# The first batch's layer norm in two halves, with new orders for the engines' instruction lists

## The reference, cut to what matters

```python
q, k, v = xn @ Wq.T, xn @ Wk.T, xn @ Wv.T
attn = softmax((q @ k.T) * tril / sqrt(512))     # masked scores are 0, not -inf: they count in the sum
gates = softmax(xn @ Wg); the 2 largest of 8, renormalized
out = x + attn @ v + sum over e of gate[e] * (xn @ We[e] + be[e])
```

## Time and profile before

| what | value |
|---|---|
| median of 3 runs | 120.28 us |
| profiled execution | 120.22 us |
| its span | 118.5 us |
| granted TensorE clock | 1.00 of full speed, throughout |
| busy TensorE matmul / weight load | 112.7 / 103.5 us |
| busy VectorE / ScalarE / GpSimd | 106.4 / 99.0 / 91.3 us |

### The profile page before, as it was taken

One profiled execution on the slowest core, in us unless ns is written; L12 is line 12 of the kernel. 1 busy time (PEld: TensorE's weight loads), 2 busy tenths in 40 slices (PEclk: granted clock), 3 DMA queues, 4 the chain that ended last, 5 costly groups with the idle time before them and its releaser, 6 DMA issues.

```text
span 118.5 us, 2933 instructions
## 1 busy us (share of the span) xinstructions
PE 112.7 (95%) x733; PEld 103.5 (87%) x733; DVE 106.4 (90%) x532; ACT 99.0 (84%) x338; POOL 91.3 (77%) x183
## 2 busy tenths in 40 slices
PE   4986999999999999999999999999999999999990
PEld 4965879998999989998899989999899989899990
DVE  0689999989999899999999899999999898998892
ACT  2456899899897999899997989899997989978930
POOL 7349569899768996699768995799868995896970
PEclk9999999999999999999999999999999999999999
DMA  3759500000300011000300020000300030000033
GB/s 95 255 165 304 157 3 6 0 3 3 89 0 3 0 55 39 0 0 3 94 3 0 0 68 20 6 0 3 94 0 0 0 90 4 0 3 0 6 91 89
DMA packets 9233, 5.18 MB, mean 44 GB/s; under 512 B 384, under 2 KB 9088, under 8 KB 9216
## 3 DMA queue, kind: packets, MB, share of 16 engines
q1 hardware_dynamic: 8656, 4.66, 13.6%
q10 hardware_dynamic: 560, 0.33, 1.0%
HBM read 2.89 MB, written 2.10 MB: 42 GB/s over the span
## 4 chain that ended last, share of the span: by engine, by line
PE 87%; DMA 4%; ACT 3%; DVE 2%; SPq 1%; issue 1%; DVEq 0%
PE ring L248 15%; PE ring L252 14%; PE ring L249 14%; PE attb L306 13%; PE score L293 8%; PE score L252 4%; PE score L249 4%; PE score L248 4%; DMA w_f<-in_w_stacked_dram 4%; PE ring L324 3%; PE ring L345 2%; PE attb L358 1%; PE ring L335 1%; PE ring L337 1%; PE ring L334 1%; ACT c_s L906 1%
## 5 line engine op out<-in xcount | busy, mean ns | idle before, releaser
L922 ACT ACTIVATE ysc<-ring,gate 128x128 f32<-128x128 f32 x124 | 35.6, 388 | 0.8 <-PE ring L252 0.6
L248 PE MATMUL ring<-w_hi,xT_hi 128*128 128x512 f32 (+2 forms) x96 | 35.5, 370 | 0.4 <-ACT xT_hi L1001 0.4
L249 PE MATMUL ring<-w_lo,xT_hi 128*128 128x512 f32 (+2 forms) x96 | 32.5, 339 | 0.0
L252 PE MATMUL ring<-w_hi,xT_lo 128*128 128x512 f32 (+2 forms) x96 | 32.5, 338 | 0.0
L1130 POOL TENSOR_TENSOR ysc<-ysc,mix 128x256 f32<-128x256 f32 x31 | 22.9, 738 | 6.2 <-DVE mix L576 3.6
L1127 POOL TENSOR_TENSOR ysc<-ysc 128x256 f32<-128x256 f32 x31 | 22.8, 736 | 6.0 <-ACT ysc L922 6.0
L576 DVE SCALAR_TENSOR_TENSOR mix<-ring,gate,mix 128x128 f32<-128x128 f32 x65 | 22.4, 347 | 0.9 <-PE ring L252 0.3
L306 PE MATMUL attb<-c_s,probT 128*128 128x128 f32 x152 | 21.8, 274 | 0.0
L306 PEld LDWEIGHTS attb<-c_s,probT 128*128 128x128 f32 x152 | 20.1, 191 | 0.2
L248 PEld LDWEIGHTS ring<-w_hi,xT_hi 128*128 128x128 f32 x96 | 18.1, 189 | 2.1 <-ACT xT_hi L1001 0.6
L252 PEld LDWEIGHTS ring<-w_hi,xT_lo 128*128 128x128 f32 x96 | 18.1, 188 | 1.5 <-DVE xT_lo L509 0.2
(11 more groups left out here) (115 smaller groups left out, 237.8 us busy)
## 6 DMA issues: line engine op xcount, KB each, us to landing
x_all<-in_x_dram SPq DMA_DIRECT2D x7, 256.0 KB, 3.9
out_dram<-o_s SPq DMA_DIRECT2D x7, 256.0 KB, 2.3
w_f<-in_w_stacked_dram SPq DMA_DIRECT2D x1, 256.0 KB, 4.5
w_f<-in_w_stacked_dram SPq DMA_DIRECT2D x1, 192.0 KB, 4.4
w_f<-in_w_stacked_dram SPq DMA_DIRECT2D x1, 132.0 KB, 3.7
x_all<-in_x_dram ACTq DMA_DIRECT2D x1, 128.0 KB, 2.7
x_all<-in_x_dram SPq DMA_DIRECT2D x1, 128.0 KB, 2.5
wqk_s<-in_w_attention_dram ACTq DMA_DIRECT2D x1, 128.0 KB, 3.9
```

The source lines that it names most:

```text
L248: nc.tensor.matmul(dst, hi, w_h, start=True, stop=False)
L249: nc.tensor.matmul(dst, hi, w_l, start=False, stop=False)
L252: return nc.tensor.matmul(dst, lo, w_h, start=False, stop=True)
L922: last = nc.scalar.mul(ysc[:, t, e, :], bank(f"A{t}", b)[:, e * P:(e + 1) * P], gate[:, b % 2, t, e:e + 1])
```

## The change

First batch: `normal_finish(0)` becomes `first_finish(0)` after tiles 0 and 1 and `first_finish(1)` after tiles 2 and 3. Each aggregates two tiles and adds EPS to two columns. GpSimd's power becomes two powers of two columns each (`first_rstd`). VectorE normalizes tile 0 before it makes the low part of the C weights and tiles 1 to 3 behind it; tiles 0 and 1 need only the first power. The negated mean of batch 0, which nothing read, is no longer made. The same diff gives new orders to all four lists and to the ring's groups; in the first part that moves, among others, `wb_high` to the front of ScalarE's list, two of batch 1's statistics ahead of `x_lo_half(0, 1)`, `u_hi(0)` ahead of `c_copy(0, 1)`, and `bias_rhs_split` ahead of `wa_low` on GpSimd. The instructions are otherwise the same. The diff, without the last parts of VectorE's and ScalarE's lists:

```diff
--- before.py
+++ after.py
@@ -53,8 +53,8 @@
 
 
 FIRST_GROUPS = """C0@0 C1@0 U@0 C2@0 C3@0 SV@0 B0@0 A0@0 X@1 A1@0 B1@0 U@1 C0@1 A2@0 C1@1 C2@1""".split()
-GROUPS = "B2- C3 A3- B3- SV DT- B0 A0 X+ A1 B1 U+ C0+ C1+ A2 C2+".split()
-LAST_GROUPS = """B2@-2 C3@-1 A3@-2 B3@-2 A0@-1 B0@-1 DT@-2 B1@-1 B2@-1 A1@-1 A2@-1 B3@-1 SV@-1 DT@-1 A3@-1""".split()
+GROUPS = "B2- C3 A3- B3- SV DT- A0 B0 X+ A1 B1 U+ C0+ C1+ A2 C2+".split()
+LAST_GROUPS = """B2@-2 C3@-1 A3@-2 B3@-2 A0@-1 DT@-2 B0@-1 B1@-1 A1@-1 B2@-1 B3@-1 A2@-1 SV@-1 A3@-1 DT@-1""".split()
@@ -398,14 +398,13 @@
             wide(0, "C", 3)
             value_sums(0)
             scores(0, 0)
+            wide(0, "B", 0)
             scores(0, 1)
-            wide(0, "B", 0)
             scores(0, 2)
             wide(0, "A", 0)
             transpose_x(1)
             transpose_probs(0, 0)
             wide(0, "A", 1)
-            transpose_probs(0, 1)
             scores(0, 3)
             wide(0, "B", 1)
             project_u(1)
@@ -413,25 +412,26 @@
             wide(0, "A", 2)
             attend(0, 0)
             wide(1, "C", 1)
+            transpose_probs(0, 1)
             wide(1, "C", 2)
 
             for n in range(1, B - 1):
                 wide(n - 1, "B", 2)
                 wide(n, "C", 3)
+                scores(n, 0)
                 attend(n - 1, 1)
-                scores(n, 0)
                 transpose_probs(n - 1, 2)
                 wide(n - 1, "A", 3)
+                wide(n - 1, "B", 3)
                 transpose_probs(n - 1, 3)
-                wide(n - 1, "B", 3)
+                scores(n, 1)
                 attend(n - 1, 2)
                 value_sums(n)
-                scores(n, 1)
                 transpose_rows(n - 1)
                 attend(n - 1, 3)
                 bias(n - 1)
+                wide(n, "A", 0)
                 wide(n, "B", 0)
-                wide(n, "A", 0)
                 scores(n, 2)
                 transpose_probs(n, 0)
                 transpose_x(n + 1)
@@ -439,43 +439,43 @@
                 wide(n, "B", 1)
                 scores(n, 3)
                 project_u(n + 1)
+                transpose_probs(n, 1)
                 wide(n + 1, "C", 0)
+                wide(n + 1, "C", 1)
                 attend(n, 0)
-                transpose_probs(n, 1)
-                wide(n + 1, "C", 1)
                 wide(n, "A", 2)
                 wide(n + 1, "C", 2)
 
             wide(B - 2, "B", 2)
+            transpose_probs(B - 2, 2)
             wide(B - 1, "C", 3)
+            attend(B - 2, 1)
             scores(B - 1, 0)
-            transpose_probs(B - 2, 2)
             wide(B - 2, "A", 3)
             wide(B - 2, "B", 3)
             transpose_probs(B - 2, 3)
             wide(B - 1, "A", 0)
             scores(B - 1, 1)
+            attend(B - 2, 2)
+            scores(B - 1, 2)
             transpose_probs(B - 1, 0)
+            transpose_rows(B - 2)
             wide(B - 1, "B", 0)
-            attend(B - 2, 1)
-            scores(B - 1, 2)
-            transpose_rows(B - 2)
+            wide(B - 1, "B", 1)
             scores(B - 1, 3)
-            wide(B - 1, "B", 1)
-            attend(B - 2, 2)
+            wide(B - 1, "A", 1)
             wide(B - 1, "B", 2)
             attend(B - 2, 3)
-            wide(B - 1, "A", 1)
+            wide(B - 1, "B", 3)
             bias(B - 2)
+            transpose_probs(B - 1, 1)
+            transpose_probs(B - 1, 2)
             wide(B - 1, "A", 2)
-            wide(B - 1, "B", 3)
-            transpose_probs(B - 1, 1)
             value_sums(B - 1)
-            transpose_probs(B - 1, 2)
+            wide(B - 1, "A", 3)
+            attend(B - 1, 0)
             transpose_probs(B - 1, 3)
-            attend(B - 1, 0)
             transpose_rows(B - 1)
-            wide(B - 1, "A", 3)
             attend(B - 1, 1)
             attend(B - 1, 2)
             bias_early(B - 1)
@@ -499,10 +499,18 @@
                     last = nc.vector.bn_aggr(mv[:, t, :], stats[:, t, :])
                 chain.step(last)
 
-                if b > 0:
-                    dve.wait_ge(S["rstd_ready"], b)
+                dve.wait_ge(S["rstd_ready"], b)
                 nc.vector.tensor_scalar_add(veps[:], mv[:, :, 1], EPS).then_inc(S["veps_ready"], 1)
                 nc.vector.tensor_scalar(nmean[:], mv[:, :, 0], -1.0, None, ALU.mult).then_inc(S["nmean_ready"], 1)
+
+            def first_finish(h):
+
+                dve.wait_ge(S["stats_ready"], 2 * h + 2)
+                for t in (2 * h, 2 * h + 1):
+                    last = nc.vector.bn_aggr(mv[:, t, :], stats[:, t, :])
+                chain.step(last)
+                two = slice(2 * h, 2 * h + 2)
+                nc.vector.tensor_scalar_add(veps[:, two], mv[:, two, 1], EPS).then_inc(S["veps0_ready"], 1)
 
             def split_lo(dst, src, hi, done):
 
@@ -703,6 +711,18 @@
 
             early, late = slice(0, 2 * P), slice(2 * P, NT * P)
 
+            def c_low(b):
+
+                dve.wait_ge(S["wc_ready"], 1)
+                split_lo(w_lo[:, c_cols], w_f[:, c_cols], w_hi[:, c_cols], S["wcl_ready"])
+
+            def xn_first(b, t):
+
+                if t % 2 == 0:
+                    dve.wait_ge(S["rstd_ready" if t else "rstd_early"], 1)
+                nc.vector.tensor_scalar(xn[:, t, :], tile_ap(0, t), mv[:, t, 0:1], rstd[:, t:t + 1], ALU.subtract,
+                                        ALU.mult).then_inc(S["xn0_ready"], 1)
+
             def a_low(b):
 
                 dve.wait_ge(S["ah_ready"], 1)
@@ -729,38 +749,37 @@
                 if t % 2 == 0:
                     dve.wait_ge(S["x0_late" if t else "x0_early"], 16)
                 normal_stats(0, t)
-            normal_finish(0)
-            dve.wait_ge(S["wc_ready"], 1)
-            split_lo(w_lo[:, c_cols], w_f[:, c_cols], w_hi[:, c_cols], S["wcl_ready"])
-            dve.wait_ge(S["rstd_ready"], 1)
-            for t in range(NT):
-                nc.vector.tensor_scalar(xn[:, t, :], tile_ap(0, t), mv[:, t, 0:1], rstd[:, t:t + 1], ALU.subtract,
-                                        ALU.mult).then_inc(S["xn0_ready"], 1)
-
+                if t % 2:
+                    first_finish(t // 2)
+            xn_first(0, 0)
+            c_low(0)
+            xn_first(0, 1)
+            xn_first(0, 2)
+            xn_first(0, 3)
             a_low(0)
             x_lo_half(0, 0)
             first_sums(0)
+            normal_stats(1, 0)
+            normal_stats(1, 1)
             x_lo_half(0, 1)
-            normal_stats(1, 0)
-            token_sums_pairs(0)
-            normal_stats(1, 1)
             normal_stats(1, 2)
             normal_stats(1, 3)
+            token_sums_pairs(0)
+            token_sums_later(0)
             normal_finish(1)
-            token_sums_later(0)
             u_lo(0)
             gate_max(0)
+            mask_scores(0, 0)
             gate_drop(0)
-            mask_scores(0, 0)
+            negate_max(0, 0)
             mask_scores(0, 1)
             gate_below(0)
-            negate_max(0, 0)
+            sv_rows(0, 0)
             negate_max(0, 1)
-            sv_rows(0, 0)
+            gate_sum(0)
             sv_rows(0, 1)
-            gate_sum(0)
+            gate_rec(0)
             sv_rows(0, 2)
-            gate_rec(0)
             gate_out(0)
             mix_b(0, 0, 0)
             mix_b(0, 0, 1)
@@ -775,108 +794,108 @@
                 negate_max(n - 1, 2)
                 mix_b(n - 1, 1, 2)
                 u_lo(n)
+                mask_scores(n - 1, 3)
                 normal_stats(n + 1, 0)
                 normal_stats(n + 1, 1)
                 normal_stats(n + 1, 2)
-                mask_scores(n - 1, 3)
+                negate_max(n - 1, 3)
                 mix_b(n - 1, 2, 0)
                 mix_b(n - 1, 2, 1)
-                negate_max(n - 1, 3)
+                mask_scores(n, 0)
                 mix_b(n - 1, 2, 2)
                 gate_max(n)
-                normal_stats(n + 1, 3)
                 gate_drop(n)
                 softmax_sum(n - 1)
+                normal_stats(n + 1, 3)
+                softmax_tot(n - 1)
                 token_sums_pairs(n)
-                softmax_tot(n - 1)
-                token_sums_later(n)
                 gate_below(n)
                 normal_finish(n + 1)
+                token_sums_later(n)
+                softmax_rec(n - 1)
+                negate_max(n, 0)
                 mix_b(n - 1, 3, 0)
-                mask_scores(n, 0)
+                gate_sum(n)
                 mix_b(n - 1, 3, 1)
-                gate_sum(n)
-                negate_max(n, 0)
+                gate_rec(n)
                 mix_b(n - 1, 3, 2)
-                gate_rec(n)
-                softmax_rec(n - 1)
                 gate_out(n)
                 mask_scores(n, 1)
                 sv_rows(n, 0)
                 sv_rows(n, 1)
+                finish_tile(n - 1, 0)
+                sv_rows(n, 2)
                 mix_b(n, 0, 0)
-                sv_rows(n, 2)
```

(38 more changed lines are left out.)

65 lines of the change are left out of this document (33 added, 32 removed).

## The result

The changed kernel takes 120.82 us (median of 5 runs, 120.65 to 121.02), the kernel before 120.28 in the same five rounds. The ratio is 1.0048 with a 95% interval of 1.0033 to 1.0063: slower by 0.4 to 0.76 us, outside the range given and on the other side.

What follows compares the result with a forecast made beforehand. TensorE was taken to bound each loop turn (13.23 us), leaving gains only at the front. Terms 0 + 0 + 0.03 + 0.37 + 0 + 0 = 0.40 us gave 119.88 us; the range was 119.6 to 120.5.

Steps and rivals of the forecast that it cites:

- Normalizing batch 1, and A1: First part: batch 1 normalized at 12.05 instead of 12.54, A1 0.03 us earlier; bounds 0.2 earlier or 0.1 later.
- From A1 on: From A1 to batch 0's B2: stalls of 0.43 us lose their causes; gain 0.37 us, bounds 0.1 and 0.43.
- The halves: Front, first batch normalized in two halves: gain 0, hidden by the A weights' DMA, which holds ScalarE until 6.84.
- the rival with an earlier landing: Front: halves bring the first C group forward if the A weights land earlier; up to 0.4 us more, 119.5, chance 0.04.
- signs that the prediction named for being wrong: First C matmul before 7.6 or after 7.95, sv_rows(0, 2) after 15.1, TensorE idle before SV, C2 or S3 each turn.
- ScalarE's front: ScalarE's start, wb_high ahead of a_high: value 0, upper bound 0.2 us later if the B weights land 0.2 later.
- The x_lo half, U: First part, x_lo_half(0, 1) behind two statistics: 0.22 us lost at U, SV and scores(0, 0) 0.2 to 0.5 earlier.
- The loop: Turns of the loop, new order of SV, DT and score groups: value 0, TensorE busy 13.23 of 13.23 us.
- The last part: End of the kernel, A3 moved forward by PT3 and attend(7, 0): value 0, bounds 0.25 less and 0.2 more.
- The power and the port: Front, GpSimd's two powers: 0.8 us each, the first ending between 4.8 and 5.3, the second between 5.6 and 6.3.
- the rival that the port holds their neighbours: Front: C weights' low part and normalizing tiles wait for the second power; gain only 0.2 us, 120.1, chance 0.05.
- a stall in each turn: Loop rival: SV waits for its sums on VectorE; 0.14 us a turn gives 120.7, slower from 0.07, chance 0.13.

Runs made afterwards that it cites:

- e17: Halves alone plus the piece of VectorE's new first-part list behind u_lo(0) (second sv_rows and gate reciprocal behind the exponential): 120.23 us, 1.0019 of the kernel before.
- e18: Halves alone plus the piece of VectorE's new first-part list ahead of u_lo(0) (x_lo half behind two statistics, token sums later): 120.23 us, 1.0019 of the kernel before.
- e6: Changed kernel with sv_rows(0, 1) in front of gate_sum(0) and gate_rec(0) behind sv_rows(0, 2): 120.53 us, 1.0027 of the kernel before.
- e7: Changed kernel with the edits of e5 and e6 together: 120.50 us, 1.0032 of the kernel before.
- e1: Kernel before with the two halves alone, every other order as before: 119.80 us against 120.25, ratio 0.9974.
- e14: Halves alone plus GpSimd's new first-part list (bias split ahead of the A weights' low part): 119.88 us, 0.9974 of the kernel before.
- e9: Halves alone with both x_hi_half ahead of wa_high on ScalarE and the bias split ahead of wa_low on GpSimd: 119.99 us, 0.9984 of the kernel before.
- e10: Kernel before, no halves, with x_hi_half ahead of wa_high and the bias split ahead of wa_low: 120.38 us, 1.0023 of the kernel before.
- e11: Halves alone with GpSimd's wb_low behind batch 1's power and TensorE's B0 behind scores(0, 2): 120.42 us, 1.0032 of the kernel before.
- e15: Halves alone plus TensorE's new first-part list (B0 ahead of scores(0, 1), second transpose of probabilities behind batch 1's C1): 120.97 us, 1.0068 of the kernel before.
- e16: Halves alone plus ScalarE's new first-part list (wb_high ahead of a_high): 120.02 us, 0.9994 of the kernel before.
- e3: Kernel before with the changed loop alone (four lists and GROUPS): 120.23 us against 120.25, ratio 0.9993.
- e5: Changed kernel with token_sums_pairs(0) in front of normal_stats(1, 2) instead of behind normal_stats(1, 3): 120.73 us, 1.0050 of the kernel before.
- e13: Halves alone plus VectorE's whole new first-part list, other engines' lists unchanged: 120.87 us, 1.0063 of the kernel before.
- e12: e9 with GpSimd's wb_low behind batch 1's power and TensorE's B0 behind scores(0, 2): 120.87 us, 1.0063 of the kernel before.

## Why the prediction was wrong

**The step that failed: "Normalizing batch 1, and A1".** It set a gain ahead of the exponential (inputs half a microsecond earlier) against a loss behind it (one sv_rows and a reciprocal), and came out at 0.03. The loss was sized right: 0.78 - 0.22 = 0.56 us in e17's rows, against 0.35 and a reciprocal of 0.18. The gain did not come. The prediction moved `wb_low` to 9.4 to 10.4 (it ran 9.41 to 10.43) and bounded the hold at 0.35 us, as if it could fall only on EPS, the operation held in the earlier trace rows. But the change also put the token sums between the statistics and EPS, and they are small operations of the same kind. The hold caught the first of them, for 0.93 us, and 0.71 us of VectorE's queue lay between the end of `w_lo` (10.43) and the end of EPS (11.14). In the kernel before that was 0.02. The right count is not when EPS could be issued, but what is queued between the held operation and EPS. `w_lo` came 0.66 us earlier (11.09 to 10.43), the queue gave 0.69 back, the power started 0.02 later. A1 came 0.59 later instead of 0.03 earlier, and that with a rounding 0.35 earlier than before; counted from the rounding it came 0.94 later. e18 and e17 show the two terms by themselves.

The sum of the bounds was wrong too. The normalizing could be 0.40 late by the prediction's own count (12.45 for 12.05), but `sv_rows(0, 2)` was given 15.0 at most. With 0.40 it is 15.27, and A1's bound is 0.37 late and not 0.1. Measured were 12.56 for the normalizing and 15.49 for the end of `sv_rows(0, 2)`.

**"From A1 on", 0.37 us.** From A1 to B2 it takes 20.57 - 15.55 = 5.02 us in the changed kernel. In the timeline of before it is 20.13 - 14.96 = 5.17, so 0.15 was won, not 0.37. In the timeline of before no row between A1 and B2 names a releaser: the 0.43 us I called stalls are spread over six places of 0.05 to 0.11 us, mostly between a group's first and second matmul. A1's first two matmuls start 0.33 us apart before and 0.34 after the change, where the earlier trace rows have 0.23. In every one of the twenty traces these two are 0.33 to 0.35 apart, whatever came before them; hand-overs that come earlier do not remove that. Where A1 came early although TensorE's and ScalarE's lists were the new ones (e6, A1 at 14.88, e7, A1 at 14.78), A1 to B2 took 5.23 and 5.24: nothing was won there at all.

**The halves, 0.** A gain of 0.3 us in e1 and again in e14 (0.9974 both). The prediction said that ScalarE's rounding of the A weights at 6.84 hides them. That part holds: from the rounding to A1 the halves change nothing (8.12 us with and without), and where nothing hides them (e9 against e10) they bring A1 0.2 us forward. What failed is the fixed 6.84. In the profiled run of e1 it begins at 6.21, and all of the front is 0.63 earlier: A1 at 14.33 for 14.96. The page shows the A weights' DMA landing after 3.9 us (e1) and 4.1 (changed kernel) instead of 4.5. Counting the profiled runs that round them ahead of the transposes' copies, the rounding begins between 6.84 and 6.99 in four of four without the halves, between 6.14 and 6.54 in nine with them, and at 6.60 to 6.99 in four more with them (e11, e15, e16, e18). e10, without the halves, has a landing after 4.0 us on its page, so an early one does not need them. The landing seems to differ between executions of one kernel as well: the profiled runs of e11, e15, e16, e17 and e18, with the rounding at 6.54 to 6.99, lie 0.34 to 0.56 us above their medians, the other eight with halves (6.14 to 6.51) within 0.21 of theirs. So in the traces the halves' gain is the earlier landing. Why the kernels with halves seem to have it in most runs (their medians are lower, e1 and e14), and what sets it, stays open. The diff does not touch these DMAs, and the rival with an earlier landing had 0.04. The first C matmul at 7.54 (7.78 before) and `sv_rows(0, 2)` at 15.49 are two of the signs that the prediction named for being wrong (before 7.6, after 15.1). One thing no run tests: in e1 the copy of the last two tiles' transposes waits 0.21 us for TensorE and starts at 7.35, and before these transposes end at 7.41 only. With the A weights as early as in e1 the kernel without halves might lag behind them.

**ScalarE's front, 0, bound 0.2 late.** In the changed kernel `wb_high` ran from 5.74 to 6.25 and held nothing: `a_high` at 6.32 follows TensorE's product of the attention weights (5.49 to 6.30 on the chain), and the A weights' rounding follows `a_high` at 6.49, 0.12 after the landing (2.27 + 4.1 = 6.37). Alone it cost 0.2 us in e16, not told from nothing by its interval.

**The x_lo half, U.** 0.22 us late at U was counted. From the A weights' rounding on it is 9.27 - 6.49 = 2.78, before 9.29 - 6.84 = 2.45: 0.33. TensorE had room for it: before, SV (11.36) waited for its sums (11.25), with the copy of C1 done at 9.73. In the changed kernel the sums end at 10.65 and the copy of C1, now behind `u_hi`, at 10.68, and SV starts at 10.75, 0.61 earlier.

**The loop, 0.** Right: e3 lies within its interval of nothing. In the trace five turns took 0.16 more, 0.1 of it in one turn (68.47 - 55.12 = 13.35 against 67.83 - 54.60 = 13.23 before); e3 has the same turn at 13.34. But five turns of the old loop take from 66.19 to 66.36 us in the other traces (66.20 in that of before), so the 66.36 is no price of the new one.

**The last part, 0, at most 0.2 more.** Within its bounds, but not 0: 0.15 to 0.19 us in the five traces with the new last part, of which 0.13 to 0.14 lie between the last matmul and the end of SyncE's issues. The prediction looked at VectorE's last operation, which is 0.04 nearer to that matmul now (0.51 and 0.55). The first of the last three stores is issued at 116.34, 0.22 before VectorE's last operation begins, where it was 0.40 before (115.50), and the other two queue behind it.

**The power and the port.** The two powers ended at 5.18 and 6.21, as forecast (before 5.3 and before 6.3); the rival that the port holds their neighbours did not occur: VectorE's `w_lo` took 0.43 us from 5.48 on, inside the second power. The Trainium skill's page "SBUF — State Buffer", the section "Who interferes with whom", says the blocked side waits for a whole instruction, and that an operation of VectorE with at most one SBUF input outside its two-port modes does not contend. The trace agrees for GpSimd's `w_lo`: the addition with two SBUF inputs took 0.93 us and ended with it, while the aggregations of before (9.95, 0.38 us) ran through the beginning of `w_lo` (10.09) unheld. For the power it does not agree, as the prediction says. Had I asked of every operation of the new list that could meet `w_lo` whether it can be held, and not only of the one seen held, the hold on the sums would have been in the term.

Of the rivals the slower one (a stall in each turn) did not happen: the change is slower by another mechanism, in the first part. The range of 119.6 to 120.5 was too narrow because the bound of A1, 0.1 late, came from a hold on EPS alone and was added up 0.27 short; 0.37 late at A1 and the lower bound of 0.1 for the stretch behind it would have given 120.55.

## What to carry to other kernels

When an operation is seen held by a long one of another engine, moving the long one does not move the end by itself: list everything that now falls under it, and count the queue between the first held operation and the one that somebody waits for. Put that one directly under the hold, not behind it. Operations moved behind a wait that ends late (here the gate's exponential) cost their full length. A stretch that is longer than the sum of its pitches need not have stalls to win: of 0.43 us that no row gave a releaser for, 0.15 went at best. And when traces differ in when the first weights land, count from there before you compare.

## What the runs showed that was not expected

A hold moves on rather than goes away: 0.75 us on EPS, 0.93 on the first sum, 0.66 (e5), 0.88 (e13) and 0.94 (e18) on the second, all ending within 0.05 us of GpSimd's end. GpSimd's low part of the A weights does it too: in e9, e10, e12 and e14 the first sum takes 0.68 to 0.73 us and ends within 0.01 us of it. The power of two columns takes 0.71 and 0.87 us, of four 1.02: halving the columns saves 0.15 to 0.31 us. The landing of the A weights moves the time by more than the whole change does: it comes 3.8 to 4.7 us after its issue in the twenty profiled runs, and e1 and e16, with roundings 0.78 us apart (6.21 and 6.99), have profiled times 0.81 apart (119.77 and 120.58). The best version of this work is the halves with the old order of the first part, 119.80 us, 0.9974 (0.9957 to 0.9992) of the kernel before.
